# Value matmuls of narrow diagonal steps, done one step later together with those of the next step

## What is computed

```python
q = (x @ Wq).reshape(B, C, H, D).transpose(0, 2, 1, 3)
...
scores = jnp.einsum('bhqd,bhkd->bhqk', q, k)
causal = jnp.tril(jnp.ones((C, C), dtype=bool))
scores = jnp.where(causal, scores, -jnp.inf)
attn = jax.nn.softmax(scores / jnp.sqrt(jnp.float32(E)), axis=-1)
ctx = jnp.einsum('bhqk,bhkd->bhqd', attn, v)
ctx = ctx.transpose(0, 2, 1, 3).reshape(B, C, E)
return ctx @ Wo + bo
...
x = x + _L0_attn_ref(_layernorm(x, axis=-1), ...)
x = x + _L0_ffn_ref(_layernorm(x, axis=-1), ...)
```

## Time and profile before

| what | value |
| --- | --- |
| median of the runs | 2180.89 us (2176.3 to 2182.03, 3 runs) |
| the profiled execution | 2181.16 us, span 2179.4 us |
| busy, share of the span | PE 93%, DVE 80%, ACT 61%, POOL 36% |
| chain that ended last | PE 71%, DVE 16%, ACT 3% |
| value matmuls (L1236) | 593.9 us busy, 20% of the span on the chain |
| granted clock of PE, mean | 0.977 of full speed |

### The profile page before, as it was taken

The page is one execution under the profiler, slowest core; times in us unless marked ns, Lnnn a source line. Parts: engine busy times, 40 slices in busy tenths (PEclk is TensorE's granted clock), DMA queues, the critical chain, the costliest instruction groups (busy, mean ns, idle before and its releaser), DMA issues.

```text
span 2179.4 us, 35926 instructions
## 1 busy us (share of the span) xinstructions
PE 2017.8 (93%) x12037; PEld 787.9 (36%) x12037; DVE 1733.4 (80%) x4370; ACT 1337.5 (61%) x2881; POOL 788.8 (36%) x1077
## 2 busy tenths in 40 slices
PE   2789999999999999999999999999999999999973
PEld 1323333333333343433434343343433333333432
DVE  5597877868986878788797887877888888889754
ACT  1136767666665667666675766666676666666640
POOL 4323233241233525334433444535232332323232
PEclk8799999999999999999999999999999999999986
DMA  2442130404031141412313141131304030210111
GB/s 92 122 121 59 45 101 29 111 26 111 6 83 41 54 111 39 120 38 54 92 43 84 46 106 52 46 110 40 109 4 106 4 103 6 78 32 6 52 41 41
DMA packets 180756, 139.75 MB, mean 64 GB/s; under 512 B 56406, under 2 KB 180572, under 8 KB 180572
## 3 DMA queue, kind: packets, MB, share of 16 engines
q1 hardware_dynamic: 180572, 137.45, 22.7%
HBM read 85.73 MB, written 50.86 MB: 63 GB/s over the span
## 4 chain that ended last, share of the span: by engine, by line
PE 71%; DVE 16%; ACT 3%; issue 3%; POOL 2%; SPq 2%; DMA 1%; POOLq 0%; ACTq 0%; DVEq 0%
PE psum L1236 20%; PE psum L1219 19%; PE psum L1204 16%; PE psum L1278 7%; DVE max_parts L960 6%; PE psum L1271 5%; DVE psum L955 3%; PE psum L1261 2%; ACT probs L808 2%; SPq L545 1%; PE psum L1254 1%; ACT acc_sb L815 1%; DVE out_shop L1127 1%; DMA shop<-in_L_attn_x 1%; PE psum L1300 1%
## 5 line engine op out<-in xcount | busy, mean ns | idle before, releaser
L808 ACT ACTIVATE probs<-psum 128x512 f32<-128x512 f32 (+3 forms) x2560 | 1226.0, 539 | 666.5 <-PE psum L1219 657.0
L960 DVE TENSOR_REDUCE max_parts<-psum 128x1 f32<-128x512 f32 x1536 | 969.9, 684 | 169.1 <-PE psum L1204 165.8
L1219 PE MATMUL psum<-q_rows,k_rows 99*128 99x512 bf16 (+3 forms) x2560 | 856.1, 351 | 3.8 <-ACT probs L808 2.3
L1204 PE MATMUL psum<-k_rows,q_rows 96*128 96x512 bf16 (+3 forms) x2560 | 818.0, 349 | 32.3 <-DVE max_parts L960 16.7
L1236 PE MATMUL psum<-probs,v_in 128*17 128x512 f32 (+3 forms) x5120 | 593.9, 536 | 13.2 <-ACT acc_sb L815 11.2
L955 DVE CUSTOM_DVE_ANT_0 psum<-psum,causal 128x128 f32<-128x128 f32 (+3 forms) x1024 | 478.8, 518 | 145.1 <-PE psum L1204 140.1
L1219 PEld LDWEIGHTS psum<-q_rows,k_rows 99*128 99x128 bf16 x2560 | 236.8, 97 | 637.0 <-ACT probs L808 489.2
L648 POOL TENSOR_SCALAR_AFFINE_SELECT probs<-probs 128x512 f32<-128x512 f32 x256 | 164.1, 641 | 826.2 <-ACT probs L808 826.2
L1204 PEld LDWEIGHTS psum<-k_rows,q_rows 96*128 96x128 bf16 x2560 | 244.5, 98 | 293.6 <-DVE max_parts L960 81.7
L1236 PEld LDWEIGHTS psum<-probs,v_in 128*17 128x17 f32 x5120 | 86.0, 95 | 232.1 <-issue 155.5
L955 DVE DVE_READ_ACCUMULATOR2_ANT max_parts<- 128x1 f32 x1024 | 146.1, 143 | 0.0
(11 more groups left out here) (116 smaller groups left out, 1354.5 us busy)
## 6 DMA issues: line engine op xcount, KB each, us to landing
qk_scratch<-shop SPq DMA_DIRECT2D x64, 384.0 KB, 2.8
q_rows<-qk_scratch SPq DMA_DIRECT2D x384, 64.0 KB, 2.4
k_rows<-qk_scratch SPq DMA_DIRECT2D x384, 64.0 KB, 2.4
shop<-in_L_attn_x SPq DMA_DIRECT2D x18, 512.0 KB, 4.3
v_scratch<-shop SPq DMA_DIRECT2D x16, 544.0 KB, 3.9
v_in<-v_scratch SPq DMA_DIRECT2D x64, 136.0 KB, 2.3
ctx_scratch<-ctx_out SPq DMA_DIRECT2D x64, 128.0 KB, 1.7
out_shop<-ctx_scratch SPq DMA_DIRECT2D x56, 128.0 KB, 3.2
```

The costliest lines, as they stand in the source:

```text
L808: nc.scalar.activation(probs[s % NPROBS][:, h, a:CHUNK], bank[SCORE_BANKS[n % 3]][:, a:CHUNK], ACT.Exp, scale=SCALE).then_inc(probs_ready, 1)
L960: nc.vector.tensor_reduce(max_parts[k % 2][:, first:first + heads, t % TILES, c], ring_bank(UNIT_USE[n])[:, 0:heads * width] .rearrange("p ...
L1204: ins = nc.tensor.matmul(dst[:, i * width:(i + 1) * width], q_rows[u][0:ROWS, qc, first + i, t % TILES * P:(t % TILES + 1) * P], k_rows[u] ...
L1219: nc.tensor.matmul(bank[SCORE_BANKS[n % 3]][:, a:CHUNK], k_rows[u][0:ROWS + LEVELS, h, kb * P:(kb + 1) * P], q_rows[u][0:ROWS + LEVELS, qc ...
```

## The change

A table says for each slot which steps' values are done in it. A step still has its values two slots behind its scores, but some have them three slots behind, in the same visit as the next step's: in chunk qc 0 the steps j = 0 and 2, in the other chunks the diagonal steps j = 1, 2 and 3. In chunk qc 0 the partner is the diagonal step j + 1, in the others the full step that follows. `values` itself, its waits and its increments are the same, and so are all other engines' programs.

```diff
@@ -61,6 +61,13 @@
+VALUES_AT = {}
+for s, (k, kb) in enumerate(STEPS):
+    j = kb - TILES * QCS[k]
+    joins_next = j in (0, 2) if QCS[k] == 0 else j > 0
+    VALUES_AT.setdefault(s + 2 + joins_next, []).append(s)
@@ -1349,8 +1356,8 @@
                         scores(p, h)
                     for n in share(units, h, HG):
                         unit(n)
-                    if h == 1 and 0 <= p - 2 < NS:
-                        values(p - 2)
+                    for s in VALUES_AT.get(p, []) if h == 1 else []:
+                        values(s)
                 items(p)
```

## The result

The changed kernel takes 2204.63 us (median; 2203.37 to 2205.64), the kernel before 2180.89 us beside it. The ratio is 1.0111, with an interval of 1.0097 to 1.0125: 24 us slower. The forecast was 2167 us with a range to 2184, so sign and range were both wrong; slower by more than 0.3% had a chance of 0.07.

What follows compares the result with a forecast made beforehand. The prediction took PE to bound the kernel mostly (71% of the chain, DVE 16%). Chunks qc 1, 2, 3 and 0 gave 6.3 + 2.1 + 2.6 + 3.2 = 14.2 us: 2181.2 - 14.2 = 2167 us, range 2148 to 2184.

Steps and rivals of the forecast that it cites:

- 0.19: PE time in us that one visit less was said to be worth, bounds nothing and 0.23.
- Rivals 3 and 4: In joined visits between steps: a 0.095 us weight load, 2177 us, chance 0.06; PE still empties, 2181 us, chance 0.04.
- w: Weight of a joined step's moved passes on PE: 0.88, 0.67, 0.46 and 0.24 us for widths 512 to 128.
- (0.19 + w) where the chain is on PE in A, less w where it is on PE in B: Rule for a joined pair's worth, for example 1.6 us for j 1 of chunk qc 1.
- A slots: Slots that lose their visit; each was to give 0.19 + w where the chain is on PE.
- B slots: Slots that get the moved passes, one slot later; each was to pay w where the chain is on PE.
- give ACT and DVE time: Said of projection and output items in chunk qc 1's slots, whose forecast gain was 6.3 us.
- 4 and 6 us of air: DVE's idle time in the two middle chunks of one head group, where it is busy 84%.
- Number 5: Rival: off-chain pairs pay w when ACT and DVE run dry in joined visits; 8.4 us slower, 2190 us, chance 0.07.
- Number 2: Rival: saved time goes into waits for score and unit banks; about 3 us remain, 2178 us, chance 0.11.
- 5.8 us of gain: Terms for chunk qc 3, 2.6 us (half the rule's 5.2), and chunk qc 0, 3.2 us.
- The 0.2 us at the accumulator's copy of chunk qc 0: Gain per group at chunk qc 0's first step, whose visit waits for ACT's copy: 0.2 x 16 = 3.2 us.

Runs made afterwards that it cites:

- mid_chunks: The changed kernel with only the 96 joined pairs of chunks qc 1 and qc 2 kept: 2203.70 us, 1.0113 of the kernel before.
- full_pairs: The kernel before with only full steps 10 and 12 of chunk qc 3 joined with the next, 32 pairs: 2185.18 us, 1.0019 of before.
- ahead_of_scores: The changed kernel with each joined visit moved ahead of head 0's score of its slot, after the previous slot's items: 1.0290 of the kernel before.

## Why the prediction was wrong

**Right.** 176 visits go, and a joined one is entered and left once. From first matmul to the next score the pair 384 and 512 takes 1.64 us on the timeline, against 0.77 + 0.99; with one going in less (0.09) that is 0.21 us, where 0.19 was said. Rivals 3 and 4, a weight load between the steps or a PE that empties there, are out: there are 464 visits, and in the joined ones the second step's first matmul stands w behind the first step's (medians 0.44 us for j 2 and 0.66 for j 1). Neither passes nor steps show the 0.095 us of a load between them: at width 384 the second pass starts 0.34 us behind the first, and the next step 0.32 behind that (medians of the 48 such visits ahead of a full step). What PE does in the 0.2 us that one way in and out costs, no run shows. PE's wait for the accumulator's copy fell from 11.2 to 7.7 us; under 7 was said. Moving the passes into the next slot costs w there: 83 us in all, as weighed.

**The step that failed** is the one that made everything else: "(0.19 + w) where the chain is on PE in A, less w where it is on PE in B". A visit on the chain was taken to be worth its whole length. It is worth no more than the slack of what comes next in line, and in the middle chunks this was about a third of what the sum said; in our pair it was 0.10 of 0.87 us. For the 96 pairs of chunks qc 1 and 2 the sum had the A slots give 47.9 us (12 x 0.86 and so on) and the B slots take 39.5, a gain of 8.4. A gave 17.6 us and B took 43.3: a loss of 26 us by slots, 23 to 25 by mid_chunks. Nearly all of the error is A's 30 us. The sentence that items "give ACT and DVE time" left out the other side. Items take banks of the same ring, so PE meets DVE at them too; in our pair the first item after the vanished visit finds its bank full. Over all pairs the items have 14 us of the added waits, scores and units 54.

The slack was to be had from the trace of before. The visit of the earlier trace rows at 1658.47 ended at 1659.24, and DVE's first full maximum began at 1658.79, so the bank that the transposes need came free for PE at about 1659.63 (1658.79, 0.69 for one maximum, and the 0.15 that PE needs from its end to its own start in the changed kernel). They started at 1659.91. The difference, 0.3 us, is the most that a visit of 0.87 us there could give. The second four transposes have less: their bank came free 0.60 later, at 1660.23, and they started at 1660.35. That leaves 0.12 us, and 0.10 came. I read DVE's busy share of the stretch (84%, "4 and 6 us of air") for it, and air elsewhere in a chunk is no slack in this place. I also misread the chain: between 1654.98 and 1697.70 it leaves PE not only for a copy of the accumulator, but for two exponentials just ahead of it (0.46 us at 1676.28, 0.34 at 1676.78).

**The rivals.** Number 5 had the right sign and about a third of the size, 8.4 us for 23.7. It charged only the pairs off the chain; the pairs on it lost most of their gain too. Its counter-argument, that four full units in the ring are 2.7 us of DVE's work and outlast the visit, doesn't hold: in our pair DVE runs dry behind the joined visit and idles 1.32 us ahead of 1680.45, where it idled 0.67 us behind the single one before. And a full ring is just what stops PE ahead of a joined visit. Number 2 named the mechanism (waits at score and unit banks in the place of the visits), and gave it a floor at no loss. This is what was left out: a wait that replaces the removed work in A does not go away in B, where the passes are paid a second time. The two were one mechanism, and their prices add: -33 us of switches, +59 us of waits. "If by 30, rival 2", I wrote of the waits; they rose by about 59.

Chunks qc 3 and qc 0 came out even where 5.8 us of gain was forecast. PE's waits rose by 11.5 and 4.4 us in them. That fits the reasons given there, DVE and the score banks, but no run takes these chunks apart by engine. The 0.2 us at the accumulator's copy of chunk qc 0 did not show: the 16 pairs with j 0 became 3.3 us longer, and all pairs of qc 0 sum to -0.6 us.

## What to carry to other kernels

Work on the engine that sets the pace can be cover for the ones that empty its buffers. Before moving it, ask at both ends: when would the engine, arriving earlier, find its next buffer free (this is the most that can be won), and is what arrives at the new place paid in full. A chain of waits says which work is on the path, not what it is worth; the worth is read off the timeline, from the release of the next wait. Work that feeds no other engine stands best, by these runs, spread between the work that does: every version with the full work that gathered it was slower or no faster.

## What the runs showed that I had not expected

Extra work can be nearly free in a kernel whose PE is busy 92%: 28 us of matmuls for about 4 us. Making ACT lighter alone didn't make the change any better (28 us of loss, 24 without), since DVE still stops PE. In the two places where full_pairs took a visit out of a wait for a DMA, PE stood 2.03 and 2.28 us, where it had stood 0.91 and 0.93, the granted clock fell from 1.00 to 0.50, and together they lost 6.6 us. Whether the visit had kept the clock up, two places don't show. And a copy that stands behind one exponential in ACT's queue couples the place of a value visit with the bank of a transpose, which had a part in the 38 us that ahead_of_scores takes over the changed kernel, with no instruction added.
